# A macaron layer with an S4 kernel: row operations, statistics and weight sums moved on VectorE, and the kernel's row made from an even and an odd part

## The reference

```python
x = x + 0.5 * ffn(layernorm(x))
x = x + s4(layernorm(x))          # along the last axis, length 512
x = x + 0.5 * ffn(layernorm(x))

def ffn(x):                        # the same weights both times, inner width 1376
    g, u = qlinear(x, gate), qlinear(x, up)
    return qlinear(silu(g) * u, down)
def qlinear(x, q, scale, A, B):    # 4-bit weights with a low-rank part of rank 32
    return x @ ((q - 7.5) * scale * 0.005).T + 0.02 * (x @ A @ B)
def s4(u):
    K = ifft(at_roots, 512).real   # at_roots: four Cauchy sums over 64 states
    return causal_convolution(u, K) + D * u
```

## Time and profile before

| | |
|---|---|
| median of 3 runs | 574.86 us (574.78 to 575.20) |
| the profiled execution, its own time | 574.97 us |
| its span in the trace | 573.1 us |
| granted clock of PE | 0.999 |
| tile 0 ends, tile 1 begins on PE | about 88.0 us |
| tile 1 ends, tile 2 begins on PE | 162.72 us |

### The profile page before, as it was taken

One profiled execution on the slowest core, in us unless ns is written; L12 is line 12 of the kernel. 1 busy time (PEld: TensorE's weight loads), 2 busy tenths in 40 slices (PEclk: granted clock), 3 DMA queues, 4 the chain that ended last, 5 costly groups with the idle time before them and its releaser, 6 DMA issues.

```text
span 573.1 us, 12244 instructions
## 1 busy us (share of the span) xinstructions
PE 560.1 (98%) x4660; PEld 433.6 (76%) x4660; DVE 410.7 (72%) x803; ACT 307.3 (54%) x751; POOL 228.4 (40%) x248
## 2 busy tenths in 40 slices
PE   7999999999899999999999999999999999999996
PEld 7544765437588877888778887788877888788975
DVE  5678984884689958799578994588845987555544
ACT  5676324754257841588415882178831676246611
POOL 4439400123015970268602695037830377014410
PEclk9999999999999999999999999999999999999999
DMA  8993402005241192001900019000291103540002
GB/s 262 366 333 117 74 15 76 3 1 99 41 22 8 21 162 38 6 2 20 184 15 6 2 36 173 15 2 2 53 155 52 37 2 63 77 157 1 2 2 74
DMA packets 87555, 39.76 MB, mean 69 GB/s; under 512 B 75881, under 2 KB 81001, under 8 KB 87497
## 3 DMA queue, kind: packets, MB, share of 16 engines
q1 hardware_dynamic: 86681, 38.84, 30.6%
q10 hardware_dynamic: 816, 0.14, 0.1%
HBM read 16.42 MB, written 4.19 MB: 36 GB/s over the span
## 4 chain that ended last, share of the span: by engine, by line
PE 91%; DVE 6%; issue 1%; ACT 1%; DVEq 1%; DMA 1%; ACTq 0%
PE banks L1504 35%; PE banks L1419 27%; PE banks L1479 11%; PE banks L1463 5%; PE banks L1636 5%; PE banks L1371 2%; PE banks L1440 1%; PE banks L1457 1%; DVEq L884 1%; DMA X<-in_x 1%; PE banks L1625 1%; PE banks L1656 1%; DVE ring L1034 0%; ACT p_stack L655 0%; DVE X L1037 0%
## 5 line engine op out<-in xcount | busy, mean ns | idle before, releaser
L1504 PE MATMUL banks<-xT,w 128*128 128x256 f16 (+1 forms) x1848 | 222.9, 273 | 0.0
L1504 PEld LDWEIGHTS banks<-xT,w 128*128 128x128 f16 (+1 forms) x1848 | 182.2, 100 | 20.8 <-DVE work L993 0.7
L1419 PE MATMUL banks<-dw,hT 128*128 128x256 f16 (+3 forms) x1408 | 183.7, 286 | 0.0
L1419 PEld LDWEIGHTS banks<-dw,hT 128*128 128x128 f16 (+1 forms) x1408 | 135.4, 98 | 34.6 <-issue 0.9
L993 DVE SCALAR_TENSOR_TENSOR work<-banks,work 128x512 f32<-128x512 f32 (+1 forms) x88 | 60.7, 689 | 55.6 <-PE banks L1463 25.3
L496 POOL TENSOR_TENSOR rstd<-veps,minus_half 128x1 f32<-128x1 f32 x32 | 20.2, 632 | 174.1 <-DVE veps L887 174.0
L1479 PE MATMUL banks<-xT,w 128*128 128x512 f16 (+1 forms) x336 | 79.1, 379 | 1.4 <-DVE work L993 0.7
L564 POOL TENSOR_SCALAR hT<-work 128x512 f16<-128x512 f32 x60 | 38.1, 635 | 87.8 <-DVE work L993 87.8
L567 POOL TENSOR_TENSOR hT<-work,hT 128x512 f16<-128x512 f32 x60 | 70.6, 1177 | 5.0
L1479 PEld LDWEIGHTS banks<-xT,w 128*128 128x128 f16 (+1 forms) x336 | 33.1, 100 | 40.8 <-ACT work L704 2.0
L574 POOL TENSOR_TENSOR z<-zs,z 128x1024 f16<-128x1024 f32 (+1 forms) x24 | 46.8, 1960 | 25.1 <-ACT z L729 25.1
(11 more groups left out here) (182 smaller groups left out, 700.1 us busy)
## 6 DMA issues: line engine op xcount, KB each, us to landing
out_x<-X SPq DMA_DIRECT2D x16, 256.0 KB, 2.5
X<-in_x SPq DMA_DIRECT2D x1, 2048.0 KB, 15.5
ring<-in_gate_q_t SPq DMA_DIRECT2D x2, 768.0 KB, 9.6
hT<-in_up_q_t SPq DMA_DIRECT2D x2, 768.0 KB, 11.2
X<-in_b SPq DMA_DIRECT2D x2, 560.0 KB, 11.1
X<-in_x SPq DMA_DIRECT2D x4, 256.0 KB, 5.5
X<-in_x SPq DMA_DIRECT2D x1, 1024.0 KB, 10.2
ring<-in_down_q_t SPq DMA_DIRECT2D x1, 1024.0 KB, 12.2
```

The lines of the kernel that those rows point to most:

```text
L1419: last = mm(acc(j)[:, 1 - c, 0:width], hT[0:rows[m], m, a, j * P:(j + 1) * P], dw[0:rows[m], m, src], start=(m == 0 and a == 0), stop=(m = ...
L1504: last = mm(dst[0:r, 0:HH], w[:, blocks + k, cols], xT[:, a, 2 * op + k, :], start=(first and k == 0 and a == 0), stop=(k == 1 and a == 1) ...
```

## The change

The row K on PE: the tables of cosines and sines, 512 columns each, are replaced by 257 columns of cosines (t = 0 to 256) and 255 of sines (t = 1 to 255). The even part takes two matmuls of 257 columns and one more, with a single row of the table; the odd part takes two of 255. ACT copies only the odd part; DVE copies the even part, writes even - odd backwards to t = 511 to 257, and adds the odd part to t = 1 to 255. These three operations stand in s4_row_scale in front of the four that were there.

On DVE, in the end of a tile: conv_stats leaves down_add. Those of sub-tiles 0 and 2 stay where they were in time; those of sub-tile 1 go behind p_sum(n+1, 2). s4_row_scale goes from behind p_sum(2, 2) to in front of p_sum(2, 1), and s4_row_split from behind pd_split(1, 3) to in front of down_read(1, 2). In tile 0, weight_sum 1 goes from in front of pd_split(0, 0) to in front of down_read(0, 3), and weight_sum 2 from behind down_add(0, 1) to behind down_add(0, 3).

On PE: the first block of a tile from 2 on waits for the last p_sum in place of the last p_split.

```diff
--- before.py
+++ after.py
@@ -206,7 +206,10 @@
         omega = view(ring, 2048, P, 3, L // 2)
         den, dsq, res = (view(ring, at, P, 2, L // 2) for at in (2816, 3328, 3840))
 
-        tab = view(ring, 0, P, 2, 2, L)
+
+        MID = L // 2
+        tab, tab_mid = view(ring, 0, P, 2, L), view(ring, 2 * L, 1, MID + 1)
+        k_odd = view(ring, 4096, 1, MID - 1)
 
         k_row, k_pad = view(ring, 4352, 1, L), view(ring, 5120, 1, 2, P + L, dt=F16)
 
@@ -263,6 +266,7 @@
         s_cauchy = sem("s4_cauchy_mm")
         s_fold = sem("s4_coefficients_folded")
         s_row = sem("s4_kernel_row_mm")
+        s_odd = sem("s4_kernel_odd_part_copied")
         s_rcopy = sem("s4_kernel_row_copied")
         s_pad = sem("s4_kernel_row_split")
         s_kscale = sem("s4_kernel_scale_everywhere")
@@ -462,11 +466,10 @@
                 if n == 0:
                     sp.wait_ge(s_dcast, M)
                     for k in range(2):
-                        for c in range(2):
-                            first = int(k == 0 and c == 1)
-                            sp.dma_start(tab[first:P, c, k, :], tab_d[c, k * P + first:(k + 1) * P, :])                                .then_inc(s_tab, 16)
-
-                    sp.dma_start(tab[0:1, 1, 0, :], tab_d[0, L // 2:L // 2 + 1, :]).then_inc(s_tab, 16)
+                        at = slice(k * P, (k + 1) * P)
+                        sp.dma_start(tab[:, k, 0:MID + 1], tab_d[0, at, 0:MID + 1]).then_inc(s_tab, 16)
+                        sp.dma_start(tab[:, k, MID + 1:], tab_d[1, at, 1:MID]).then_inc(s_tab, 16)
+                    sp.dma_start(tab_mid, tab_d[0, MID:MID + 1, 0:MID + 1]).then_inc(s_tab, 16)
                 if n + 1 == FAST:
                     kernel_toeplitz()
                 if n > TILES:
@@ -814,7 +817,7 @@
                     p_high(n + 1, 0)
                 if s4:
                     act.wait_ge(s_row, 1)
-                    nc.scalar.activation(k_row, bank[3][0:1, :], ACT.Copy).then_inc(s_rcopy, 1)
+                    nc.scalar.activation(k_odd, bank[3][0:1, MID + 1:], ACT.Copy).then_inc(s_odd, 1)
                 pd_copy(n, 1)
                 if more:
                     p_high(n + 1, 1)
@@ -1035,8 +1038,6 @@
                                        dtmp[:, b, :], ALU.mult, ALU.add).then_inc(f.dsum, 1)
                 dve.wait_ge(f.dsum, k + 1)
                 V.tensor_tensor(X[:, s, :], X[:, s, :], dsum[:, :], ALU.add).then_inc(f.x_out, 1)
-                if n < TILES and j < 3:
-                    conv_stats(n, j)
 
             def conv_stats(n, j):
 
@@ -1109,7 +1110,6 @@
                 if n == 0:
                     s4_inverse()
                     down_b()
-                    weight_sum(1, 0, 1)
                 fast = more and n + 1 >= FAST
                 pd_split(n, 0)
                 down_read(n, 0)
@@ -1120,6 +1120,10 @@
                     p_split(n + 1, 0)
                 down_read(n, 1)
                 down_add(n, 0)
+                if n < TILES:
+                    conv_stats(n, 0)
+                if s4:
+                    s4_row_scale()
                 if fast:
                     p_sum(n + 1, 1)
                 if more:
@@ -1128,30 +1132,34 @@
                 down_add(n, 1)
                 if fast:
                     p_sum(n + 1, 2)
-                if n == 0:
-                    weight_sum(2, 0, 1)
-                if s4:
-                    s4_row_scale()
+                if n < TILES:
+                    conv_stats(n, 1)
                 if c is not None:
                     conv_add(c * TS)
                     conv_add(c * TS + 1)
                 if more:
                     p_split(n + 1, 2)
+                if s4:
+                    s4_row_split()
                 down_read(n, 2)
                 down_add(n, 2)
+                if n < TILES:
+                    conv_stats(n, 2)
                 if c is not None:
                     conv_add(c * TS + 2)
                 pd_split(n, 3)
-                if s4:
-                    s4_row_split()
                 if fast:
                     p_sum(n + 1, 3)
                 if more:
                     p_split(n + 1, 3)
                 if c is not None:
                     conv_add(c * TS + 3)
+                if n == 0:
+                    weight_sum(1, 0, 1)
                 down_read(n, 3)
                 down_add(n, 3)
+                if n == 0:
+                    weight_sum(2, 0, 1)
 
             def low_rank_b(part, g):
 
@@ -1278,7 +1286,13 @@
 
             def s4_row_scale():
 
+
+                dve.wait_ge(s_odd, 1)
+                turned_row = bass.AP(k_row.tensor, k_row.offset + L - 1, [list(k_row.ap[0]), [-1, MID - 1]])
+                V.tensor_copy(k_row[:, 0:MID + 1], bank[3][0:1, 0:MID + 1])
+                V.tensor_tensor(turned_row, bank[3][0:1, 1:MID], k_odd, ALU.subtract).then_inc(s_rcopy, 1)
                 dve.wait_ge(s_rcopy, 1)
+                link(V.tensor_tensor(k_row[:, 1:MID], k_row[:, 1:MID], k_odd, ALU.add))
                 link(V.tensor_tensor(k_row[:, 0:1], k_row[:, 0:1], d_first[:, :], ALU.add))
                 link(V.tensor_reduce(k_row_scale[:, 0:1], k_row, mybir.AxisListType.X, ALU.max,
                                      apply_absolute_value=True))
@@ -1514,7 +1528,7 @@
                     if m == 0:
                         for j in range(2):
                             pe.wait_ge(f.xTq[j], 32 * (n - FAST + 1))
-                        pe.wait_ge(f.p_stack, (n + 1) * TS)
+                        pe.wait_ge(f.p_sum, (n - FAST + 1) * TS)
                         if n == FAST:
                             pe.wait_ge(s_wsum, 8)
                             pe.wait_ge(s_rcopy, 1)
@@ -1620,10 +1634,13 @@
 
                 pe.wait_ge(s_fold, 1)
                 pe.wait_ge(s_tab, 80)
+                even, odd = bank[3][0:1, 0:MID + 1], bank[3][0:1, MID + 1:]
                 for k in range(2):
-                    for c in range(2):
-                        last = mm(bank[3][0:1, :], fold[:, 4 + c, k:k + 1], tab[:, c, k, :],
-                                  start=(k == 0 and c == 0), stop=(k == 1 and c == 1))
+                    mm(even, fold[:, 4, k:k + 1], tab[:, k, 0:MID + 1], start=(k == 0), stop=False)
+
+                mm(even, fold[0:1, 5, 0:1], tab_mid, start=False, stop=True)
+                for k in range(2):
+                    last = mm(odd, fold[:, 5, k:k + 1], tab[:, k, MID + 1:], start=(k == 0), stop=(k == 1))
                 last.then_inc(s_row, 1)
 
             def conv_product(i):
```

## The result

The changed kernel takes 573.20 us (median of 8 runs, 573.12 to 573.24), beside 574.92 (8 runs, 574.75 to 575.20) for the kernel before on the same chip: a ratio of 0.9969, 95% interval 0.9959 to 0.9980. That is 1.7 us off, for the 2.2 that were forecast, inside the range. The span went from 573.1 to 571.2 us. The profiled executions lie 1.85 us apart (574.97 and 573.12).

The account below looks back on a forecast made before the run. PE, busy 98% of the span, was taken to bound the kernel, so only less PE work or fewer waits help. 1.18 + 1.11 - 0.05 = 2.24 us off gave 572.6 against 574.86; range 571.8 to 573.8.

Parts of the forecast that it names:

- Tile 0: End of tile 0: with both weight sums moved, PE stops waiting for the pd_stack split; gain 1.18 us.
- The row on PE: End of tile 1: fewer matmul columns cut the S4 row on PE from 3.60 to 2.25 us, 1.35 less.
- The three operations: End of tile 1, before p_sum(2, 1): new one-partition DVE copy, backward difference and sum take 1.26 us, bounds 0.85 and 2.06.
- rival (2): Backward write and single partition are dear: the three new DVE operations take 2.06 us, time 573.4; chance 0.09.
- rival (5): The three new DVE operations are held, 2.08 us each; tile 1's end loses 3.87, time 577.6; chance 0.04.
- The chain behind them: End of tile 1: DVE, without pause from p_sum(2, 1) to p_sum(3), decides; tile 2 starts 1.11 us earlier.
- rival (4): End of tile 1: DVE is quicker than counted and PE decides; time 572.3, chance 0.08.
- p_sum for p_stack: Start of tile 2: waiting on p_sum instead of the last p_split gains 0.05 us, bounds nil and 0.1.
- Tiles 2 and 3: p_sum(n+1, 2) waits for PE before the statistics, delaying them and the first conv_add; 0.05 us lost for both tiles.
- all later tiles begin as much earlier: From tile 2 on: tile 2 begins 2.2 to 2.4 us earlier, and so do all later tiles.
- a tile 2 that starts early and a tile 4 that does not: Sign that would show the prediction wrong: tile 2's early start is lost by tile 4; no size given.
- Rival (1): Tile 1's DVE and POOL collision does not shift as a whole: one wait more or less, 573.3 or 571.9; chance 0.09.

Follow-up runs that it names:

- run 1: The kernel before with only the two weight sums of tile 0 moved; 573.92 us, ratio 0.9980.
- run 4: The changed kernel with the four old row operations behind p_sum(2, 1), the three new ones still in front; 572.55 us, ratio 0.9957.
- run 5: The changed kernel with the wait for p_stack at the start of a tile restored; 573.21 us, ratio 0.9970.
- run 2: The kernel before with three more tiny DVE memsets at its start; 575.64 us, ratio 1.0011.
- run 3: The changed kernel with three of the four small memsets at the start done by GpSimd instead of DVE; 572.37 us, ratio 0.9952.
- run 9: The changed kernel with the four old row operations behind p_sum(2, 1) and three start memsets on GpSimd; 572.79 us, ratio 0.9962.
- run 10: The changed kernel with the four old row operations behind p_sum(2, 1) and all four start memsets on GpSimd; 571.91 us, ratio 0.9947.
- run 8: The kernel before with only the statistics of sub-tile 1 moved behind p_sum(n+1, 2); 574.87 us, ratio 0.9998.
- run 7: The changed kernel with the statistics of sub-tile 1 back in front of p_sum(n+1, 2); 574.25 us, ratio 0.9987.
- run 6: The changed kernel with the whole row on PE again, no new DVE row operations, three memsets keeping DVE's instruction count; 573.27 us, ratio 0.9971.

## Why the prediction was right, and where it was off

The time is 0.6 us above the forecast of 572.6. By its own steps:

- **Tile 0.** Forecast 1.18 us, measured 143.61 - 142.44 = 1.17 at the next common point. Of that 1.09 arises at the place itself, and 0.08 was there ahead of it. Run 1 shows it alone: 1.1 us. The covers for the sums were there, a little larger than reckoned: 1.04 us were left of the first, where 2.21 - 1.66 = 0.55 could be expected, and 3.75 of the second for 3.65.
- **The row on PE.** 2.43 us for 2.25, and 1.10 saved for 1.35: the forecast scaled the recorded length of 3.60, whose end overlaps the next work, and had no joints. The columns count as forecast (in the trace passes of 257 start 0.22 us apart, those of 512 started 0.43 apart), and about 0.1 goes at each of the two joints between the shapes. With DVE in front of p_sum as it is, that didn't matter.
- **The three operations.** 1.21 us for 1.26, none over 0.41: rival (2), the dear backward write, is out, and so is rival (5). By the figures of the Trainium skill, VectorE: DVE Perf Modes, section on the TRN2 errata, the prediction had an estimate of 1.20, and the trace's 1.21 agrees with it.
- **The chain behind them.** p_sum(2, 1) came at 149.45, for 150.74 - 1.17 = 149.57 forecast; the new wait of PE is 0.81, where "more than a microsecond" was said; from p_sum(1) to p_sum(3) it is 9.40 us for 9.54; the last low-rank product comes 1.08 behind that for 1.07. PE's wait is shorter than said because its row ended later than forecast. The term came out at 2.48 - 1.17 = 1.31 us, for 1.11. Run 4 shows that it is DVE that decides, which closes rival (4).
- **p_sum for p_stack.** 0.05 was counted, run 5 shows nothing. Tile 2 still starts 0.31 us behind the low-rank product (160.24 - 159.93).
- **Tiles 2 and 3.** 0.05 was counted, and it is nothing: 70.38 and 70.30 us for 70.38 and 70.29 (by the chains, starts at 160.32, 230.70 and 301.00 for 162.80, 233.18 and 303.47).
- **What was not in the sum.** At the start of tile 2 it had 2.3 us and the kernel 2.48. The step that failed is the last one, that all later tiles begin as much earlier. Tile 4 gave 0.53 back: 1.17 + 1.31 - 0.53 = 1.95, and tile 5 starts 1.94 earlier. The last tile gave back 0.07 more (record 1087), which leaves the 1.86 us of the span; the medians are 1.72 apart. The prediction did name "a tile 2 that starts early and a tile 4 that does not" as what would show it wrong, without a mechanism for it.
- **A reading.** That tiles 3 to 7 start without such a wait is not quite so: the earlier trace rows has one of 0.33 us at the end of tile 6. It stands in both kernels and changes nothing in the sum.

Rival (1) gave 573.3, the measured time to 0.1, but not for its reason. Its collision in tile 1 shifted as a whole, as the forecast had it:

```profile
111.80 2.13 POOL L577 TENSOR_TENSOR z<-zs,z 128x1024 f16<-128x1024 f32 x1 [11.09 <-ACT z L732]
111.87 2.08 DVE L1270 TENSOR_TENSOR cw<-cs,cw 128x4 f32<-128x4 f32 x1
```

The meeting of DVE and POOL that did change is in tile 4. Shown by experiment (runs 2, 3, 9 and 10): the number of DVE instructions ahead decides which length tile 4 has. The twelve traces agree: five have the h product 20.29 to 20.30 us behind the start of tile 4, and tile 4 takes 69.77 to 69.79 us (the kernel before, runs 1, 3, 8 and 10); in the other seven it is 19.94 or 19.95, and tile 4 takes 70.30 or 70.31. That the late product gets its gain by the order in which DVE and POOL then meet is read from the traces; no run changed that order by itself. What holds the one instruction is only argued. The hold is at a fixed place of the order and not at a fixed time, it recurs with 128 records, and it meets instructions that wait for nothing, which fits the loading of instructions; no run took that cause away.

What each step is worth at the end of tile 1 is best read from the length of tile 1:

| | tile 1, us |
|---|---|
| before; run 1 (sums only) | 74.62; 74.61 |
| run 8: statistics moved, row operations where they were | 74.51 |
| run 7: row operations moved (and the halves), statistics where they were | 74.29 |
| changed kernel; run 6 (whole row) | 73.32; 73.31 |
| run 4: four row operations behind p_sum(2, 1) | 72.62 |

By themselves the statistics give 0.11 us and the row operations 0.33, together 1.30. So of the 1.7 us, the weight sums are 1.1 and the two moves together 1.3, less the 0.5 of tile 4 and 0.1 of the last; that is the whole, to 0.1. Making the row in halves is worth nothing in this order (run 6).

## What to carry to other kernels

Find what decides the end of the stretch before shortening another engine's work there: 1.1 us less on PE was worth nothing, since it was paid for with 1.2 us on DVE ahead of the same p_sum, and moving four small operations behind that p_sum's addition was worth 0.65. Two moves that each give little alone can give much together, when each leaves the other's wait in place (0.11 and 0.33 us against 1.30). An instruction taken out or put in early can move a later stretch by half a microsecond either way, through the place at which an engine is held and how two engines then meet. So compare the lengths of all stages of the two traces, not only the changed one, and keep the number of instructions equal where an effect under a microsecond is to be told (run 6 did). And two gains of 0.8 and 0.65 us, measured apart, gave 0.4 together in one build and 1.3 in one that differed from it by a single memset: measure the sum.

## What was not expected of the hardware

- DVE starts an instruction late at places of its order that are 128 records apart (63, 191, 319, 575, 703, 831, 959 and 1087, counted from 0), be it an h product, an aggregation or a small operation that stands there. It is 0.34 to 0.37 us for an h product (575, 703, 831, 959, 1087), 0.36 to 0.43 for an aggregation (63, 191, 703), and only 0.14 to 0.17 for small operations of the statistics (319, 575). Not every such record is late: behind long operations nothing of it is seen (run 4, record 703), and at 191 nothing is seen in runs 3, 9 and 10 either, where a small 128x4 operation stands there.
- A late DVE instruction can make the kernel faster: with the h product 0.34 us late, tile 4 is 0.53 shorter. In tile 3 of run 9 another h product, 0.35 late, makes the tile 0.43 longer.
- Writing 255 values backwards on one partition takes 0.40 us, as much as the forward copy of 257. Four fp32 passes of 257 columns and the joint behind them take 0.96 us on PE (142.76 to 143.72), two and a joint 0.52 (143.72 to 144.24): about 0.22 a pass, and about 0.1 for the change of shape.
